# A waited-for fill of a 128x128 scratch tile behind each indirect transfer on GpSimd

## The reference

```python
# layer 0, two passes
edge = concat([h[src], h[dst]])
weighted = mlp2(edge, msg) * sigmoid(mlp2(edge, att))
h = mlp2(concat([h, segment_sum(weighted, dst)]), upd) + h + global_repr
# layer 1
agg = segment_sum(x[src], dst); batch norm over the nodes, relu, matmul
# layer 2
attn = einsum(Q[dst], K[src]) * rel_scale[edge_type] / sqrt(DH)
out = segment_sum(softmax of attn over the edges of each dst * V[src], dst)
# layer 3: scores of 8 heads from Q[dst] . K[src], edge and node terms,
# softmax over the edges of each dst, weights applied to V, projection, layer norm
```

## Time and profile before

| | |
|---|---|
| Time of the three runs | 7089.4, 7088.25, 7090.32 us; median 7089.4 |
| Span of the profiled execution | 8961.2 us |
| PE / DVE / ACT / POOL busy in it | 63% / 54% / 13% / 54% of the span |
| Mean granted TensorE clock in it | 0.674 of full speed |

### The profile page before, as it was taken

One profiled execution on the slowest core, in us unless ns is written; L12 is line 12 of the kernel. 1 busy time (PEld: TensorE's weight loads), 2 busy tenths in 40 slices (PEclk: granted clock), 3 DMA queues, 4 the chain that ended last, 5 costly groups with the idle time before them and its releaser, 6 DMA issues. The chain is left out here.

```text
span 8961.2 us, 134318 instructions
## 1 busy us (share of the span) xinstructions
PE 5673.7 (63%) x28658; PEld 4800.1 (54%) x28659; DVE 4867.9 (54%) x17338; ACT 1151.3 (13%) x3238; POOL 4865.9 (54%) x4715
## 2 busy tenths in 40 slices
PE   6555556677777767777768778656666665333334
PEld 5555555466666556666655555456666663333333
DVE  6555554455555545555557777545555553444555
ACT  1111111111111111111112222100000001000001
POOL 2566564555555355555527888445454451566664
PEclk6555555777777877777779999865655556555556
DMA  5334434333333233333324444333333332333332
GB/s 154 95 95 97 94 94 126 92 97 93 95 93 96 57 102 94 94 97 98 94 53 67 69 69 69 78 83 88 89 89 87 89 89 37 77 75 75 74 77 49
DMA packets 930244, 770.85 MB, mean 86 GB/s; under 512 B 586631, under 2 KB 762899, under 8 KB 928115
## 3 DMA queue, kind: packets, MB, share of 16 engines
q0 software_dynamic: 245936, 426.87, 19.9%
q1 hardware_dynamic: 675276, 329.60, 14.6%
q10 hardware_dynamic: 8960, 13.52, 0.6%
HBM read 681.88 MB, written 86.32 MB: 86 GB/s over the span
## 5 line engine op out<-in xcount | busy, mean ns | idle before, releaser
L1180 POOL DMA_INDIRECT there<-table_wide,idx x1664 | 1597.4, 960 | 1396.8 <-DVE prod L1203 615.9
L1271 PE MATMUL ps<-here,hot_t 128*128 x3328 | 1238.1, 507 | 631.3 <-DVE there L1222 599.7
L2288 POOL DMA_INDIRECT there<-table_wide,idx x832 | 792.7, 953 | 902.6 <-DVE msg L2364 434.8
L1222 DVE TENSOR_TENSOR there<-there,ps 128x512 f32<-128x512 f32 x832 | 571.2, 687 | 1169.8 <-remote 607.7
L1271 PEld LDWEIGHTS ps<-here,hot_t 128*128 128x128 f32 x3328 | 740.9, 247 | 756.5 <-issue 668.9
L2677 POOL DMA_INDIRECT there<-table_narrow,idx x832 | 791.3, 951 | 649.5 <-issue 259.1
L693 POOL DMA_INDIRECT rec<-out_recd,posd x806 | 817.5, 1014 | 564.4 <-issue 263.9
L1279 PE MATMUL ps<-relu,hot_s 128*128 128x128 f32 x3328 | 878.0, 356 | 140.3 <-DVE hot_s L1211 108.1
L2837 PE MATMUL ps<-here,hot_t 128*128 x1664 | 434.5, 436 | 803.6 <-DVE prod L2758 419.3
L1947 POOL DMA_INDIRECT partial_sums<-row_sums1a,idx1a x504 | 814.9, 1617 | 167.4 <-issue 147.3
L1279 PEld LDWEIGHTS ps<-relu,hot_s 128*128 128x128 f32 x3328 | 688.5, 238 | 326.3 <-issue 272.1
(11 more groups left out here) (486 smaller groups left out, 9773.3 us busy)
## 6 DMA issues: line engine op xcount, KB each, us to landing
locrows<-loc_row SPq DMA_DIRECT2D x416, 256.0 KB
krowd<-key_row SPq DMA_DIRECT2D x201, 256.0 KB
there<-table_wide,idx POOLq DMA_INDIRECT x2496
src_rows1a<-slot_src_row SPq DMA_DIRECT2D x42, 768.0 KB
lrowd<-lo_row SPq DMA_DIRECT2D x201, 128.0 KB
attr_raw<-in_edge_attr SPq DMA_DIRECT2D x201, 128.0 KB
there<-table_narrow,idx POOLq DMA_INDIRECT x832
rec<-out_recd,posd POOLq DMA_INDIRECT x806
```

Of the source, the lines that this page charges most:

```text
L1180: nc.gpsimd.indirect_dma_start(there[:, j, q, :], None, table, bass.IndirectOffsetOnAxis(idx[:, j, q:q + 1], 0)).then_inc(gathered[j][q], 16)
L1222: nc.vector.tensor_tensor(pair, pair, ps[:, WORK, :], ALU.add).then_inc(summed, 1)
L1271: last = nc.tensor.matmul(ps[:, WORK, (q % 2) * 2 * F:(q % 2 + 1) * 2 * F], hot_t[:, j % 2, q * P:(q + 1) * P], here[:, :, :].rearrange("p ...
L2288: nc.gpsimd.indirect_dma_start(there[:, j, q, :], None, table, bass.IndirectOffsetOnAxis(idx[:, j, q:q + 1], 0)).then_inc(gathered[j][q], 16)
```

## The change

A scratch tile `pause` of 128x128 float32 is allocated. Behind each of 4159 indirect transfers, POOL fills it with zeros, waits until the fill has finished, and (outside the last stage) adds one to `admitted`. These are 806 scatters of the sort, 1664 gathers of layer 0, 832 each of layers 2 and 3, and 25 fetches of the last stage. The 504 transfers of layer 1 and 7 others are as before. Nothing reads `pause`.

```diff
@@ constants
+    k["pause"] = top.sb("pause", [P, P])
@@ sort_edges
+            paused = s.sem("paused" + tag + "")
...
                         nc.gpsimd.indirect_dma_start(rec, bass.IndirectOffsetOnAxis(pos[:, j, g:g + 1], 0),
                                                      out[:, j, g, :], None).then_inc(sent[j][g], 16)
+                        nc.gpsimd.memset(k["pause"][:, :], 0.0).then_inc(paused, 1)
+                        pool.wait_ge(paused, i * (SLOTS * G) + (j * G + g + 1))
+                        pool.sem_inc(admitted, 1)
@@ attention_messages (layer 0); the same three lines in layers 2 and 3
                         pool.sem_inc(admitted, 1)
                         nc.gpsimd.indirect_dma_start(there[:, j, q, :], None, table,
                                                      bass.IndirectOffsetOnAxis(idx[:, j, q:q + 1], 0)).then_inc(gathered[j][q], 16)
+                        nc.gpsimd.memset(k["pause"][:, :], 0.0).then_inc(paused, 1)
+                        pool.wait_ge(paused, i * (RING * U) + (j * U + q + 1))
+                        pool.sem_inc(admitted, 1)
@@ last_stage
                 nc.gpsimd.indirect_dma_start(found_rows[:, t, :], None, spool, bass.IndirectOffsetOnAxis(run["pos"][:, t:t + 1], 0)).then_inc(found, 16)
+                nc.gpsimd.memset(k["pause"][:, :], 0.0).then_inc(paused, 1)
+                pool.wait_ge(paused, t + 1)
```

More of the change, by code:

```diff
@@ L1142, in attention_messages @@
         indexed = [c.sem(f"indexed{j}" + tag) for j in range(RING)]
+        paused = c.sem("paused" + tag + "")
         admitted, passed = c.sem("adm" + tag), c.sem("passed" + tag)
@@ L2636, in edge_scores @@
         order = c.sb("block_order", [1, NV], i32)
+        paused = c.sem("paused3")
         ordered, indexed, admitted = c.sem("blocks_ordered"), c.sem("indexed3"), c.sem("adm3")
@@ L2926, in last_stage @@
         inverted, returned, normed, finished = c.sem("inverted_last"), c.sem("returned_last"), c.sem("normed_last"), c.sem("finished_last")
+        paused = c.sem("paused_last")
         out_turned, out_kept, stored = c.sem("out_turned3"), c.sem("out_kept3"), c.sem("out_stored")
```

## The result

The changed kernel takes 10,520.1 us (median of 4 runs, 10,515.2 to 10,530.1); the kernel before, beside it, 7088.8 us (4 runs, 7069.9 to 7090.3). The ratio is 1.485, 95% interval 1.4829 to 1.4871: 3431 us more, or 0.825 us for each of the 4159 transfers. The forecast was 10,820.

A forecast was written before the change was run, and what follows sets the result against it. The prediction took POOL's queue of gathers to bound the unprofiled kernel, at 1.27 us a transfer. With the change, 8961 us for the stages, 1837 outside and 21 in the last stage gave 10,820 us, range 9,200 to 12,200.

The forecast's parts named there:

- What paces the runs: All five gather stages: without a profile, POOL's queue of gathers sets the pace, at 1.27 us a transfer.
- its check: Whole kernel before: 1837.2 us outside the stages plus 5190.5 if POOL never waited, 7027.7 against the measured median 7089.4.
- The restart behind the wait: POOL, each transfer behind the new wait: starts from a standstill, 0.80 us, replacing the 0.305 of issue.
- rival A: POOL's sequencer prepares the next gather during the fill; only fill and gap are added, 8,570 us; 13 in 100.
- Gap before the fill: POOL, from a gather's end to its fill: 0.15 us, the middle between 0 and 0.305.
- The fill: POOL, behind each transfer: 0.205 us, waited for, so nothing overlaps its end.
- Layer 0's steps: Layer 0, between new wait and gather: computed values and a semaphore step, 0.15 us a transfer (0 to 0.25).
- The last stage: Its 25 fetches, on the chain that ended last: 0.85 us added to each, 21 us in all.
- The increment costs nothing: The new semaphore increment on POOL has no one waiting for it and is joined to the wait: 0.
- B (fills held by DVE): Every fill on POOL is slowed while DVE works, 0.45 us more each, 12,690 us; 6 in 100.
- C (landing): A fill on POOL can't finish before its gather has landed: 3.66 us a transfer, 17,000 us; 3 in 100.
- D: Not slower: POOL has the room the profile page shows and another engine paces the runs, 7,090 us; 3 in 100.

The follow-up runs named there:

- steps without the fill: Changed kernel with each loop fill replaced by a plain semaphore increment on POOL's sequencer, nothing added in the last stage; first chip, 7080.3 us, 0.9983 of the kernel before.
- half the gathers: Kernel before with every second gather of layers 0, 2 and 3 left out, POOL raising their semaphores itself; first chip, 6438.8 us, ratio 0.908.
- One wait later: Changed kernel with two scratch tiles in turn, each loop wait asking for the fill of the transfer before; first chip, 7546.9 us, 1.0642 of the kernel before.
- increment of the last stage: Changed kernel with a semaphore increment also behind each wait in the last stage; second chip, single run, 10,551.4 us, 1.16 of the kernel before.
- a fill a group: Changed kernel with one waited-for fill per group, 618 for 4159, none in the last stage; second and third chip, 9062.3 us (0.9969) and 9072.8 us (0.9925).
- two runs of one column: Changed kernel with 128x1 fills, each waited for one transfer later; second and third chip, 9154.6 us (1.0101) and 9167.2 us (1.0025) against the kernel before.

## Why the prediction was right, step by step

**What paces the runs.** Right in its conclusion: POOL's queue does, at 1.27 us a transfer by the prediction. The first chip's profile (steps without the fill) has stages of 1049.8, 1046.1, 1046.0, 1078.3 and 1070.8 us, cut as the prediction does, together 5291 for 4134 transfers, 1.28, and half the gathers take 653 us off. Its premise was wrong: the profile looks like one of a slower chip, on which POOL did wait for DVE and ACT, and not like a stretched execution of the chip that gave 7089.4. That its check came within 62 us was partly luck: the 1837.2 us outside were 51 too large and the floor of 5190.5 was 100 too small against the 1786 and 5291 of the first chip's profile. The 1837.2 us outside the stages came from that profile and stood in a sum for the runs; the first chip's profile has 7077.1 - 5291.0 = 1786 there with the last stage, the changed kernel 1757.9 (the drains between stages are shorter: after layer 3, 13.8 where 30.2 stood). Against the changed kernel the 1837 were 84 us too large, and the 21 us of the last stage 16.

**The restart behind the wait.** Right: 0.79 in layers 2 and 3 and 0.82 in the sort, against 0.80. One wait later it is 0.16. The Trainium skill, "DMA: Bandwidth & Descriptors", section "Anatomy of one DMA", gives the sequencer's dispatch as about 50 ns, by which the sum would have been rival A's. The trace disagrees: 0.79 of idle, and some 0.6 between the sequencer's steps at 7506.2 and 7506.8 with only a gather and a fill to send.

**Gap before the fill.** Mis-sized: 0.15 taken, 0.00 measured, 4134 x 0.15 = 620 us too much. It was the lower end given.

**The fill.** 0.205 taken, 0.218 to 0.221 measured, 54 us too little; one to one in the time, as said.

**Layer 0's steps.** 0.15 taken; 0.94 and 1.02 less 0.79 are 0.15 and 0.23, 0.19 on average, 67 us too little.

**The rest of the stages.** The sum of 0.95, 0.22 and the idle is 1.96 in layers 2 and 3, 2.00 in the sort, 2.15 in layer 0; the stages took 2.05, 2.03, 2.12 and 2.20. In layer 2 the row of the group gives it: idle 803.9 less one wait of 105.3 at the stage's start is 0.84 on average, where the common restart is 0.79, and the mean gather 0.99, where the median is 0.95. The trace of layer 2 has 0.96 before the first gather of a group (7503.04), 1.38 at each turn of the loop (7420.01), nine idle times of about 2.8, and some gathers of up to 1.2. The prediction counted such waits as covered and took every gather at its median. Together they are 0.05 to 0.12 a transfer; the 310 us of the next sum are what is left over once the other terms are in, and they pay back half of the gap's error. Restarts of 0.79 for 0.80 take 33 off, the sort's 0.82 adds 16. The stages: 8961 - 620 + 54 + 67 + 310 - 33 + 16 = 8755, measured 8755.5. Stages 206 too high and the rest 100: that is the 10,820 against the span of 10,513. So the 3% owe something to luck: the gap alone was 620 too much, and the terms left out made up half of it.

**The last stage.** Mis-sized: 0.85 a fetch taken as added, 1.44 less 1.25 is 0.19; 21 us were forecast, some 5 came. The prediction didn't see that a wait directly ahead of the transfer costs less than one with a step behind it.

**The increment costs nothing.** Wrong as a reason, though not in the sum: by the last stage it turns a 0.27 idle into 0.81. The 0.80 of the prediction came from places with a sequencer step in between the earlier trace rows, which is why the sum met the loops.

**The rivals.** A (restart hidden) fell to the 1.96 spacing; it is what the kernel becomes with the wait one later, at 7547, below even its 7670. B (fills held by DVE) fell to the means of 218 to 221 ns over 4134 fills. The Trainium skill, "SBUF — State Buffer", section "Who interferes with whom", has a rule by which DVE in a two-port mode can hold up such a fill. The trace shows nothing of rival B's size: the median fill took 0.218, the longest in layer 2 0.26 and in the sort 0.48. C (landing) fell too: the fill starts with its idle of 0 and is over after 0.22, and a gather's landing takes 2.8 us in the median. D fell with the 1.485. On the second chip it is partly true: there POOL had slack, and about the same kernel (with the increment of the last stage) costs 1.16, since it takes 10,551 where the changed one took 10,520.

**Left open.** What slows the second and third chip; what a fill a group costs on a chip like the first; whether the loops without the increment run at 1.44 plus their own waits; why one fill a group shortens the sort; the 1% between the two runs of one column.

## What to carry to other kernels

A wait for the engine's own last instruction can cost far more than the instruction, when a semaphore step stands between it and the next transfer: here 0.22 us of fill cost 0.82, because the next transfer's dispatch could no longer run ahead. Asking for the instruction one earlier gave back 87% of it; in the last stage, where no step stood behind the wait, fill and wait together cost only 0.19. An engine whose busy share is 55% (the changed kernel) or 69% (the steps without the fill, where PE has 73%) can set the pace, if what lies between its instructions is dispatch: read the spacing of starts, not the share. And when the profile's span and the runs differ by a quarter, first ask whether both are of the same chip.

## What the runs showed of the hardware

One kernel took 7091.5, 9093.1 and 9134.5 us on three chips, with mean granted clocks of 0.749 to 0.753, 0.677 to 0.683 and 0.674 to 0.682; one gather's work on POOL took 0.944 to 0.949 in the median on all. Where POOL paces, the difference is gone: 10,520 us beside a kernel before of 7089, and 10,551 beside one of 9093, with the increment in the last stage as the only difference of the two kernels.

A fill behind an indirect transfer starts with no gap, a transfer behind a fill that it doesn't wait for after 0.16 to 0.19, behind a transfer after 0.30, behind a wait directly ahead of it after 0.27, and behind a wait with a semaphore step between after 0.79 to 0.82. A 128x128 fill takes 0.22, a 128x1 fill 0.11.
